# A layer step in which TensorE runs the value products ahead of the query transposes

## The reference

```python
DIM = 128; DEPTH = 6; HEADS = 16; DIM_HEAD = 64; WINDOW = 32
def attn_layer(x, Wqkv, qs, ksc, Wo):
    q, k, v = jnp.split(x @ Wqkv, 3, -1)          # then split into 16 heads
    q = l2norm(q) * qs
    k = l2norm(k) * ksc
    q = q * cos * scale + rotate_half(q) * sin * scale
    k = k * cos * inv + rotate_half(k) * sin * inv
    out = local_attention(q, k, v)                # softmax(8 q k') v over this window of 32 and the one before
    return out @ Wo
for i in range(DEPTH):
    x = attn_layer(shift_tokens(x), Wqkv[i], q_scale[i], k_scale[i], Wo[i]) + x
    x = ffn_layer(shift_tokens(x), ln_g[i], ln_b[i], W1[i], b1[i], W2[i], b2[i]) + x
```

## Time and profile before

| | |
|---|---|
| median of 3 runs | 2013.35 us (2007.73 to 2013.68) |
| span of the profiled execution | 2010.7 us |
| PE busy | 1805.9 us (90%) |
| PEld busy | 1311.9 us (65%) |
| DVE busy | 1557.0 us (77%) |
| POOL busy | 1455.2 us (72%) |
| ACT busy | 1164.3 us (58%) |

### The profile page before, as it was taken

One profiled execution on the slowest core, in us unless ns is written; L12 is line 12 of the kernel. 1 busy time (PEld: TensorE's weight loads), 2 busy tenths in 40 slices (PEclk: granted clock), 3 DMA queues, 4 the chain that ended last, 5 costly groups with the idle time before them and its releaser, 6 DMA issues. The chain is left out here.

```text
span 2010.7 us, 85596 instructions
## 1 busy us (share of the span) xinstructions
PE 1805.9 (90%) x34280; PEld 1311.9 (65%) x34280; DVE 1557.0 (77%) x2776; ACT 1164.3 (58%) x1966; POOL 1455.2 (72%) x967
## 2 busy tenths in 40 slices
PE   7774689999999999999999999999999999999995
PEld 3453466676776666766666666667676667676764
DVE  4764688887888878888788788887887888878864
ACT  2311356666666666666666666666666666666662
POOL 3221688877887778777877787778777877787771
PEclk9875899999999999999999999999999999999997
DMA  4000122223222223222223322233222232222220
GB/s 151 2 3 1 44 65 65 59 54 86 73 70 53 55 63 91 59 70 63 61 53 84 77 68 55 52 82 81 63 58 59 63 86 63 70 63 55 55 58 22
DMA packets 93581, 123.43 MB, mean 61 GB/s; under 512 B 27760, under 2 KB 41808, under 8 KB 93392
## 3 DMA queue, kind: packets, MB, share of 16 engines
q1 hardware_dynamic: 93232, 122.42, 24.2%
q10 hardware_dynamic: 288, 0.13, 0.0%
HBM read 20.74 MB, written 1.05 MB: 11 GB/s over the span
## 5 line engine op out<-in xcount | busy, mean ns | idle before, releaser
L999 POOL TENSOR_TENSOR across<-unit,turns 128x1024 f32<-128x1024 f32 x192 | 497.4, 2591 | 279.7 <-issue 268.4
L1006 POOL TENSOR_TENSOR rotated<-along,across 128x1024 f32<-128x1024 f32 x192 | 496.7, 2587 | 14.2
L1151 DVE TENSOR_REDUCE sums<-squares 128x16 f32<-128x1024 f32 x192 | 234.2, 1220 | 173.2 <-ACT squares L1054 173.1
L1247 PE MATMUL turn<-identity,rotated 128*128 128x128 f32 x1536 | 205.2, 277 | 36.4 <-POOL rotated L1006 36.4
L1247 PEld LDWEIGHTS turn<-identity,rotated 128*128 128x128 f32 x1536 | 172.6, 141 | 98.9 <-issue 83.4
L1032 POOL TENSOR_TENSOR along<-unit,turns 128x1024 f32<-128x1024 f32 x96 | 228.3, 2378 | 0.0
L1352 PE MATMUL proj_a<-w_qkv,shift_a 128*128 128x512 f32 x384 | 189.9, 617 | 36.4 <-DVE unit L1176 30.1
L1113 ACT COPY val<-proj_a 128x1024 f32<-128x1024 f32 x96 | 97.2, 1013 | 181.3 <-PE proj_a L1352 181.3
L1377 PEld LDWEIGHTS att<-o_t,w_o 128*128 128x128 f32 x1536 | 188.0, 193 | 6.1 <-issue 1.0
L1377 PE MATMUL att<-o_t,w_o 128*128 128x128 f32 x1536 | 188.3, 276 | 0.0
L1280 PE MATMUL proj_a<-w_qkv,shift_a 128*128 128x512 f32 x384 | 183.5, 601 | 4.3 <-POOL shift_a L988 3.0
(11 more groups left out here) (203 smaller groups left out, 3445.2 us busy)
## 6 DMA issues: line engine op xcount, KB each, us to landing
v_win<-val SPq DMA_DIRECT2D x1536, 64.0 KB, 2.0
w_qkv<-wqkv_dram SPq DMA_DIRECT2D x18, 512.0 KB, 3.8
w_o<-wo_dram SPq DMA_DIRECT2D x6, 512.0 KB, 4.6
where<-positions_dram SPq DMA_DIRECT2D x1, 2048.0 KB, 11.4
w_ffn<-ffn_dram SPq DMA_DIRECT2D x12, 170.5 KB, 2.3
w_ffn<-ffn_dram SPq DMA_DIRECT2D x6, 192.0 KB, 2.3
x_tok<-x_dram SPq DMA_DIRECT2D x4, 256.0 KB, 4.3
out_dram<-final SPq DMA_DIRECT2D x4, 256.0 KB, 2.4
```

Source lines behind the costliest of these rows:

```text
L999: pool.tensor_tensor(a[:, :, ::-1, :], u, table, ALU.mult).then_inc(acrossed[j], 1)
L1006: pool.tensor_tensor(rotated[j][:, :, :], along[j][:, :, :], across[j][:, :, :], ALU.add).then_inc(rotated_in[j], 1)
L1151: dve.tensor_reduce(sums[:, j, :], squares[j][:, :, :], AX.X, ALU.add).then_inc(summed[j], 1)
L1247: mm = pe.transpose(bank[:, TILE * (i % 4):TILE * (i % 4) + TILE], buffer[:, TILE * i:TILE * i + TILE], identity[:, :])
```

## The change

In PE's step the block of the value products is moved from behind the query transposes to in front of them. Nothing else is edited: the waits are those of before and move with their block, and the orders of DVE, ACT, POOL and SP are the same.

```diff
                         mm.then_inc(k_projected, 1)
-                    if live["a"]:
-                        pe.wait_ge(rotated_in[0], a + 1)
-                        after(pe, centred, 2 * a)
-                        stand_alone(pe, passed)
-                        transposes(bank_t[:, 0, :], rotated_flat[0], 0, q_turned)
-                        if live["down"]:
-                            pe.wait_ge(gated, NC_ * (h + 1))
-                        transposes(bank_t[:, 1, :], rotated_flat[0], 1, q_turned)
                     if live["b"]:
                         pe.wait_ge(p_laid, 2 * b + 2)
                         pe.wait_ge(v_spread, 256 * b + 256)
...
                                     if (a_, w) == (PAIRS - 1, BLOCKS - 1):
                                         mm.then_inc(mixed, 1)
+                    if live["a"]:
+                        pe.wait_ge(rotated_in[0], a + 1)
+                        after(pe, centred, 2 * a)
+                        stand_alone(pe, passed)
+                        transposes(bank_t[:, 0, :], rotated_flat[0], 0, q_turned)
+                        if live["down"]:
+                            pe.wait_ge(gated, NC_ * (h + 1))
+                        transposes(bank_t[:, 1, :], rotated_flat[0], 1, q_turned)
                     if live["a"]:
                         pe.wait_ge(rotated_in[1], a + 1)
```

## The result

The changed kernel takes 1979.72 us (median of 4 runs, 1978.87 to 1980.29), against 2013.33 us for the kernel before (4 runs, 2007.73 to 2013.68). The profiled execution has a span of 1978.2 us instead of 2010.7: 32.5 us less. The forecast was 22 us less (1991.3 us, range 1985 to 2006).

What follows compares the result with a forecast made beforehand. DVE was taken to bound each step at the value projection, PE right behind. A pair gains 0.23 + 0.28 us, less POOL meetings, 0.46: 20.2 us in the loop plus 1.8 outside, 22 us, giving 1991.3 us (range 1985 to 2006).

Steps and rivals of the forecast that it cites:

- What bounds the kernel: Before the value projection PE waits for DVE's `unit`, 0.23 us in even and 0.44 us in odd steps.
- The value products' start: Value products were to start g = 0.1 us behind the end of the key projection, bounded by 0 and 0.42 us.
- the bound of 0.42 us: Upper limit of g: value products lose all the early loading of first weights seen before the query transposes.
- The turn-around: ACT's query copies before key transposes: odd steps lose 0.5 us, hidden under PE's wait; even steps still wait for POOL.
- the worth of DVE's gap: DVE's idle gap before `heads_out` goes wholly, so root and `unit` come 0.27 us (even) and 0.28 us (odd) earlier.
- the 0.14 us that I gave back for a late `k_t`: Odd step before the value projection: 0.14 us taken off PE's slack, leaving 0.43 us, more than the 0.28 us needed.
- the meetings with POOL: DVE's root, moved earlier, can meet two POOL copies: 0 to 0.11 us more per step, 0.025 taken off.
- My rival "more": POOL and DVE meet less, or steps ahead of the loop gain more: 28 us gained, 1985 us; chance 0.04.
- half of it: Rival: DVE's gap closes but the root loses 0.11 us to POOL each step: 12 us gained, 2001 us; chance 0.10.
- nothing: Rival: the gap at `heads_out` returns as a wait at `unit` or the value projection: 2013 us; chance 0.02.
- the two on the turn-around: Rivals at g = 0.42, late key transposes: turn-around bounds PE, 2008 us, chance 0.10; turn-around in full, 2023 us, chance 0.06.
- the slower case: Rival: turn-around before key transposes with every term at its worst: 10 us slower, 2023 us; chance 0.06.

Runs made afterwards that it cites:

- the lengthened turn-around: Changed order with the second half of the query transposes run twice, against the kernel before: 2061.62 us, ratio 1.0261.
- the single long step: One odd step of 19.64 us instead of 18.10, in the changed order with POOL's two shifted-input copies made by ACT; that kernel took 1982.32 us, 0.9865.

## Why the prediction was right and wrong, step by step

**What bounds the kernel** was right: DVE ahead of the value projection, with PE just behind. The kernels with one kind of step changed show that each kind gains by itself, and what is left of a step without its stall and root does not move. The even gain is the 0.23 us said, the odd one 0.44 us where I had 0.28.

**The value products' start** (g = 0.1 us) measured 0.09 us. The trace also shows what the bound of 0.42 us was about: the first weights are not loaded ahead any more, and yet the first value product comes only 0.09 us late. The turn-around came out as said in odd steps: the key transposes start at 3.01 us behind the key projection (3.03 said), the output transposes at 3.99 (3.98 said).

In even steps the number is right and the reason is not. The key transposes start at 3.15 us (3.16 said), but ACT releases them and not POOL. POOL's keys are ready at 3.01 us and ACT's first copy at 3.06 (medians), where my sum put the copy's end at 2.97. The value products took 1.69 us from their start to that of the query transposes (900.43 to 902.12), and I had counted 1.61. That the two waits end within 0.05 us of each other is luck. Two small slips besides: 3.09 less 2.94 us is 0.15 and not 0.14, and the 0.59 us for one copy is not in the rows that I named (the trace of before has it, 0.59 us on average).

**The step that failed is the worth of DVE's gap.** I read it as the idle time of the row, 0.27 or 0.28 us. But `heads_out` starts 0.08 us before the sums ahead of it end when it need not wait, as it does now. From start to start the wait cost 0.36 us. In the odd step this is 0.08 us more than counted. PE had slack for all of it: the 0.14 us that I gave back for a late `k_t` did not come, since the scores start 0.16 us earlier behind the key projection than before (5.39 against 5.55 us), and 0.15 us of waiting for `unit` is left. In the even step PE's 0.23 us were the most that could be gained, as forecast, and the step gained 0.23 us.

**The second error is the sign of the meetings with POOL.** I took off 0.025 us a step for the root. It is 0.13 us longer in the even step (2.12 to 2.25), a little more than the 0.11 feared, and 0.08 us shorter in the odd one (2.20 to 2.12), which I hadn't thought of: an operation that moves can also leave a collision. In the odd step of before two operations met a copy (L90 took 0.24 us and L92 0.32), in that of the changed kernel one does (L96, 0.28). The 0.08 us are gained. The 0.13 us seem to be hidden, but only by chance: 0.36 - 0.13 = 0.23 us is what DVE gives, and 0.23 us is also PE's bound. The two ends meet within 0.02 us (PE is through with the scores 0.01 us before the value projection starts; `unit` ends 0.12 us before it, and 0.10 us where DVE alone decides). That PE alone would have stopped the even step at the same place is argued from its slack before; no run shows it by itself.

A pair then gains 0.23 + (0.36 + 0.08) = 0.67 us; measured are 0.68 us, and the loop of 44 pairs gave back 29.6 us by the starts of L1352, where the forecast had 20.2. The difference of 9.4 us is the overlap (0.08 x 44 = 3.5), the odd root (0.08 x 44 = 3.5) and the allowance of 0.05 us a pair that I took off (2.2). Outside the loop 2.9 us were gained where I had put 1.8; that part differs by several us between kernels whose loops are alike, so it says little. My rival "more" had a part of the mechanism in it (fewer meetings, in odd steps), but nothing of the 0.08 us, and I gave it no price from rows; its 1985 us were the bottom of my range.

**Of the rivals**, "half of it" and "nothing" are out, and so are the two on the turn-around, whose steps would have come to nearly the old 17.84 and 18.64. But the experiment with the lengthened turn-around showed that I had mispriced the slower case. I had taken it as 0.1 us for each 0.1 us; by what those runs show, it would have met the change of order between L1234 and L1006, only 0.18 us away, and cost 1.0 us or more in each odd step. This is argued from the kernel with the lengthened turn-around and from the single long step; the slower case itself was not run. The kernel was nearer to a large loss than my 2023 us said.

## What to carry to other kernels

A wait is worth the time from the start of the operation ahead to the start of the waiting one, less what this takes when nothing is in its way, and not the idle time in its row; take both from a place where the same engine runs through. When a chain moves by a few tenths of a microsecond, list the operations that hold each other up (here DVE's with two inputs in SBUF, and POOL's) with their distances before and after, count the meetings that are left as well as those that are made, and look for the pair whose order is decided by less than the shift. A wait that is missing in a list with a lower limit is not zero: measure from start to start on both sides before calling it new. Small products whose result is waited for go in front of work that only feeds a copy, as long as the waits behind still cover the copy.

## What the runs showed of the hardware that was not expected

- DVE's operations without a dependency overlap by 0.07 to 0.09 us in the profile, in this kernel between the sums and `heads_out`, as between the two `unit` products of before (917.06 + 1.22 = 918.28 against the next start at 918.21 in the even step of the earlier trace rows).
- The root's small operations of DVE with two inputs in SBUF mostly take 0.28 to 0.34 us instead of 0.18 or 0.19 when they start in a copy or product of POOL; L90 took 0.24 us in the odd step of before, and one that starts just ahead of a copy or near its end can keep its 0.19 us. With the copies on ACT none of them did in the order of before (root 2.03 us in both kinds of step). The Trainium skill says of GpSimd that it shares its SBUF interfaces with VectorE ("GPSIMD Engine Reference", Key points); these runs agree, and put mostly 0.09 to 0.16 us on a meeting of a small operation, and 1.9 us on that of a large one (3.10 against 1.22 us).
- With the change of the tiling behind a product of 512 columns, the first value product starts 0.09 us behind the projection. From there to the next transposes it is 1.59 us (odd steps) and 1.69 us (even), where it was 1.53 us in the odd steps of before; whether the tiling has a part in that is not shown. The Trainium skill says that such a change drains TensorE ("TensorEngine Tiling (Array Packing)", Key Properties); a drain by itself does not show in the trace. What shows is that the weights are no longer loaded early: the weight load stood idle for 0.76 us ahead of the value products, by the timeline of that part of PE in the changed kernel's even step:

```profile
900.43 1.59 PEld L1306 LDWEIGHTS att<-v_win,p_t 64*32 64x32 f32 x128 [0.76 <-issue]
```
